# Global attention: two PSUM copies move from ScalarE's queue to VectorE's

## The reference

```
q = rope((x @ Wq).reshape(b, s, 2 * H, hd)); k = rope((x @ Wk).reshape(b, s, 2 * H, hd))   # 32 half heads of 8
v = (x @ Wv).reshape(b, s, H, 2 * hd)                                                      # 16 heads of 16
probs = softmax(einsum('bhqd,bhkd->bhqk', q * hd ** -0.5, k))
w = probs[:, :, 0] - lam * probs[:, :, 1]
attn = einsum('bhqk,bhkd->bhqd', w, v)
attn = attn * rsqrt(mean(attn * attn) + EPS) * subln_g * (1 - LAMBDA_INIT)
return attn.reshape(b, s, -1) @ Wo
```

## Time and profile before

| | us |
|---|---|
| median of 3 runs | 8516.29 (8493.72 to 8532.59) |
| the profiled execution | 8488.95 |
| its span, first to last instruction | 8484.5 |
| PE, DVE, ACT, POOL busy | 7651.8 (90%), 6965.3 (82%), 6290.1 (74%), 3252.0 (38%) |
| of these: DVE's reductions L1440, 4096 | 4707.9 |
| ACT's exponentials L1515, 8192 | 4405.8 |
| ACT's copies L1524 (224) and L1530 (256) | 86.7 and 64.1 |

### The profile page before, as it was taken

The page is one execution under the profiler, slowest core; times in us unless marked ns, Lnnn a source line. Parts: engine busy times, 40 slices in busy tenths (PEclk is TensorE's granted clock), DMA queues, the critical chain, the costliest instruction groups (busy, mean ns, idle before and its releaser), DMA issues. The chain is left out here.

```text
span 8484.5 us, 166411 instructions
## 1 busy us (share of the span) xinstructions
PE 7651.8 (90%) x65584; PEld 2773.6 (33%) x65584; DVE 6965.3 (82%) x8955; ACT 6290.1 (74%) x11674; POOL 3252.0 (38%) x4567
## 2 busy tenths in 40 slices
PE   6899978999789997899988999889998899979999
PEld 3322343223432234322343223432234322343223
DVE  5899768997689976899768997689976899668996
ACT  3699756997569975699756997569975699656996
POOL 3244232442324423344233442334423344234441
PEclk9999989999899998999999999999999999989999
DMA  0100001000010000100001000010000100001000
GB/s 30 46 21 23 17 11 46 21 24 15 11 46 21 24 15 11 46 24 21 15 11 46 25 21 15 11 50 21 22 19 6 50 21 25 18 4 50 22 23 21
DMA packets 219176, 205.43 MB, mean 24 GB/s; under 512 B 108086, under 2 KB 143414, under 8 KB 218358
## 3 DMA queue, kind: packets, MB, share of 16 engines
q1 hardware_dynamic: 218364, 194.46, 8.0%
HBM read 123.83 MB, written 67.37 MB: 23 GB/s over the span
## 5 line engine op out<-in xcount | busy, mean ns | idle before, releaser
L1440 DVE TENSOR_REDUCE mfull<-ps 128x1 f32<-128x1024 f32 x4096 | 4707.9, 1217 | 328.6 <-PE ps L1362 327.7
L1515 ACT ACTIVATE work<-ps 128x512 f32<-128x512 f32 x8192 | 4405.8, 598 | 373.6 <-PE ps L1384 257.5
L1402 PE MATMUL ps<-work,vbuf 128*32 128x256 f32 x32768 | 2624.1, 392 | 119.5 <-ACT hh L1535 119.5
L1362 PE MATMUL ps<-kop,qop 48*128 48x512 bf16 x8192 | 2490.4, 385 | 47.8 <-DVE mfull L1440 24.3
L1384 PE MATMUL ps<-qop,kop 51*128 51x512 bf16 x8192 | 2488.8, 384 | 0.9 <-DMA qop<-mT 0.7
L1402 PEld LDWEIGHTS ps<-work,vbuf 128*32 128x32 f32 x32768 | 654.4, 108 | 1769.3 <-issue 968.2
L1384 PEld LDWEIGHTS ps<-qop,kop 51*128 51x128 bf16 x8192 | 481.6, 93 | 1641.3 <-ACT work L1515 1525.8
L1466 POOL CAST mpart<-mfull 128x16 bf16<-128x16 f32 x256 | 50.4, 197 | 2467.0 <-issue 2004.2
L251 POOL TENSOR_TENSOR rstd<-rstd,nhalf 128x8 f32<-128x8 f32 x64 | 109.3, 1707 | 1632.4 <-DVE rstd L245 1632.4
L1484 POOL TENSOR_TENSOR work<-work,none 128x16 f32<-128x16 f32 x224 | 650.3, 2903 | 18.8 <-POOL mpart L1470 1.5
L450 POOL TENSOR_TENSOR hh<-work,hmask 128x1024 f32<-128x1024 f32 x256 | 520.7, 2062 | 111.4 <-PE ps L382 79.0
(11 more groups left out here) (178 smaller groups left out, 8868.0 us busy)
## 6 DMA issues: line engine op xcount, KB each, us to landing
qop<-scratch SPq DMA_DIRECT2D x512, 64.0 KB
scratch<-work SPq DMA_DIRECT2D x32, 768.0 KB, 4.1
scratch<-hh SPq DMA_DIRECT2D x32, 768.0 KB, 3.6
kop<-scratch SPq DMA_DIRECT2D x256, 96.0 KB
vbuf<-in_x SPq DMA_DIRECT2D x9, 2048.0 KB, 8.3
qop<-scratch SPq DMA_DIRECT2D x512, 32.0 KB
kop<-scratch SPq DMA_DIRECT2D x256, 64.0 KB
qop<-mT SPq DMA_DIRECT2D x1024, 3.0 KB
```

The lines of the kernel that those rows point to most:

```text
L1362: pe.matmul(ps[:, b + n, :], qop[r:r + KQ, s, i, t * P:(t + 1) * P], kop[r:r + KQ, s, i, half(n)], start=True, stop=True).then_inc(s_ms, 1)
L1402: mm = pe.matmul(ps[VW * i:VW * (i + 1), OB, cols], vp[:, b, t, (G * gl + i) // 2, :], prob[:, u % PS, i, cols], start=t == 0 and part == ...
L1440: v.tensor_reduce(mfull[:, m // CUT % 2, r // ROWS * G // 2 + i, to:to + 1], ps[:, b:b + NB, :].rearrange("p b n -> p (b n)"), AX.X, ALU.m ...
L1515: act.activation(prob[:, u % PS, hl, :], ps[:, EB[slot % len(EB)], :], ACT.Exp, scale=scale).then_inc(s_ex, 1)
```

## The change

`keep_raw` and `keep_maxima` leave ACT's queue and stand in DVE's. DVE's loop over the 512 reductions becomes a loop over the clock. In a step it issues `keep_raw` (if an early turn is due), then `reduce(e + 23)`, then `keep_maxima` (if a turn of maxima is due). Early turns get a semaphore of their own, `s_rk`, since `s_ex` now counts ACT's exponentials alone: PE's `bank_for` waits for `s_rk` where the bank's last user was an early turn, and POOL's `early` waits for `s_rk` too. No instruction is removed or added but for the move; bytes, tiles and PE's order stay.

```diff
                     def bank_for(slot):
-                        if slot >= len(EB):
-                            pe.wait_ge(s_ex, slot - len(EB) + 1)
+                        last = slot - len(EB)
+                        if last in TURNS:
+                            pe.wait_ge(s_rk, TURNS.index(last) + 1)
+                        elif last >= 0:
+                            pe.wait_ge(s_ex, last + 1 - sum(1 for s in TURNS if s < last))
                         return EB[slot % len(EB)]
...
                         if part == 0:
-                            pe.wait_ge(s_ex, slot_of(G * (u + 1) - 1) + 1)
+                            pe.wait_ge(s_ex, G * (u + 1))
...
+                    def keep_raw(j):
+                        slot = turn_slot(j)
+                        if j >= 2:
+                            v.wait_ge(s_ch, LINKS * (j - 2) + 2)
+                        v.wait_ge(s_sc, slot + 1)
+                        src = ps[:, EB[slot % len(EB)], :].rearrange("p (k w) -> p k w", w=VW)
+                        v.tensor_copy(raw[j % 2], src[:, :, 0:LD + 1]).then_inc(s_rk, 1)
+
+                    def keep_maxima(h):
+                        v.wait_ge(s_mt, h + 1)
+                        if h >= 1:
+                            v.wait_ge(s_md[(h - 1) // NB % SLOTS], placed(h - 1))
+                        v.tensor_copy(mT[:, :], turn_at(h)[1]).then_inc(s_mts, 1)
+
                     project_dve(v)
-                    for m in range(LAST):
-                        reduce(m)
+                    for e in CLOCK:
+                        if e in EARLY:
+                            keep_raw(EARLY.index(e))
+                        if e + AHEAD < LAST:
+                            reduce(e + AHEAD)
+                        if at(e, TURN) is not None:
+                            keep_maxima(at(e, TURN))
...
-                        pool.wait_ge(s_ex, turn_slot(j) + 1)
+                        pool.wait_ge(s_rk, j + 1)
...
                     for e in CLOCK:
-                        if e in EARLY:
-                            keep_raw(EARLY.index(e))
                         if 0 <= e < LAST:
                             for n in range(NB):
                                 exponentials(NB * e + n)
-                        if at(e, TURN) is not None:
-                            keep_maxima(at(e, TURN))
                         if tile_due(e, 1) is not None and tile_due(e, 1) % T == T - 1:
                             keep_output(tile_due(e, 1))
```

More of the change, by code:

```diff
@@ L1238, in diff_attention @@
             s_ch = sem("da_ch")
+            s_rk = sem("da_rk")
             DMAS = 2 * (len(Q_ROWS) + len(K_ROWS))
@@ L1276, in turn_slot @@
                 return NB * EARLY[j] + j
+            TURNS = [turn_slot(j) for j in range(len(EARLY))]
             def max_bank(m):
@@ L1516, in exponentials @@
                                        ACT.Exp, scale=scale).then_inc(s_ex, 1)
[L1518 to L1530, removed]
                     def keep_output(u):
```

## The result

| | before | changed |
|---|---|---|
| median, us | 8516.07 (8493.72 to 8532.59, 4 runs) | 8663.57 (8661.13 to 8666.80, 4 runs) |
| the profiled execution, us | 8488.95 | 8666.80 |
| its span, us | 8484.5 | 8665.1 |

The ratio is 1.0175, 95% interval 1.0152 to 1.0199: slower by 147 us (129 to 169 by the interval), where 144 was forecast. That the two errors cancel to 3 us is luck.

A forecast was written before the change was run, and what follows sets the result against it. PE was taken to set the pace, with DVE and ACT close behind. The maxima's copy adds 144 us, the early copy, ACT's relief and DVE's amount nothing: 8516 + 144 = 8660 us, range 8600 to 8715.

The forecast's parts named there:

- The bound: Clocked phase: PE sets an ordinary step's pace, 1.11 us; a 16-step cut takes 19.52 us, including events in PE's order.
- Step 1: Maxima's copy behind DVE's reduction of m-1: PE's tile m 0.58 us later, 248 times, +144 us (+114 to +169).
- free by then: At the turn of the maxima, ACT was taken as free when it copies them, 1504.90 to 1505.15.
- Step 2: Early copy, 224 of them, 0.44 us each, fits DVE's hole behind the early turn: nothing, upper end +22 us.
- Step 3: ACT without the two copies, 64.1 + 86.7 us busy: it has slack already, so nothing gained.
- Step 4: DVE's load per cut becomes 18.6 us, under 19.52: not the bound by amount, only by order at one place.
- ACT as the bound: Rival: PE truly waits for ACT, so moving its copies takes 150.8 us off, median 8365 us; chance 0.05.
- Given back: Rival: PE's 0.43 us wait for DVE per turn falls away, leaving +37 us, 8553 us; chance 0.07.
- The early copy that also pushes: Rival: DVE has no hole at the early turn, each of 224 costs 0.35 us: +78 on top, 8738; chance 0.10.
- the signs named in advance: Profile after: cut 20.1 us, PE's copy waits 0.5 to 0.6, turn wait still 0.43, ACT's busy time some 150 us lower.

The follow-up runs named there:

- e1: Changed kernel with the maxima's copy given back to ACT, the early copy left on DVE: 8511.69 us, ratio to before 0.9991.
- e2: Changed kernel with the early copy given back to ACT, the maxima's copy left on DVE: 8672.65 us, ratio to before 1.0181.
- e3: Changed kernel with the maxima's copy put ahead of the reduction of m-1 in DVE's queue: 8520.24 us, ratio to before 1.0009.
- e6: Kernel before, maxima turned behind the step's value products into tile m's second bank, copy wait before the second half: 8473.63 us, ratio 0.9959.
- e5: Kernel before with an extra, unused SBUF copy in ACT's queue ahead of each maxima copy: 8661.46 us, ratio to before 1.0183.
- e4: Changed kernel, maxima turned into tile m's second bank, PE's wait for their copy before the second half: 8588.37 us, ratio to before 1.0090.
- e7: Changed kernel with the maxima copied twice in DVE's queue, first into a spare tile: 8684.89 us, ratio to before 1.0213.

## Why the prediction was right, step by step

**The bound.** It held that PE sets the pace, that DVE and ACT are near it, and that a place in a queue decides and not a sum of busy time. e1 (ACT relieved of 224 copies: nothing), e2 (the loss with 256 short copies on DVE) and e3 (all of DVE's new work and no loss) show it. PE's pace has one part that is DVE's, as the prediction said: the 0.43 us that each turn waits for the reduction of m-2, and e6 gained by filling it. The 1525.8 us of the earlier trace rows, in which PE's weight loads followed an exponential, were no waits that set the time: the row reads 1445.5 us over 3624 loads after the change, 80 us less, while the kernel became 147 us slower.

```profile
PEld ps L1390 <- ACT work L1540: 1445.5, 3624, 1.1
```

**Step 1, the maxima's copy.** Place and chain were right: the copy starts 1.13 after the reduction of m-1, at 572.27 (571.14 + 1.13); PE starts tile m 0.15 after the copy's end (572.47 to 572.62); the second half, the products, DVE's and ACT's next instructions all shift. The mis-sized term was the copy: 0.205 us, not 0.28. So a turn costs 0.49, not 0.58, and the step is 248 x 0.49 = 122 us, not 144. I had chosen the f32 row of 274 ns as the nearest and named the price that the Trainium skill gives (VectorE: DVE Perf Modes, the sections on the TRN2 errata and on the perf-mode tier table), by its formula an estimate of 0.19 us for a 16-bit copy of 128 columns from PSUM. The trace bears the page out within 0.015 us, and the sum by it was 122.

One reading of the kernel before was wrong and harmless: ACT was not "free by then". Its six exponentials run to 1501.73 + 3.28 = 1505.01, and the copy starts at 1504.90, 0.11 before that end, as ACT's exponentials do that stand back to back (0.60 less 0.49). It is 0.15 behind the turn's end (1504.53 + 0.22 = 1504.75), where the idle DVE of e3 started 0.04 behind it. So ACT's copy was held by the instruction in front of it too; that instruction holds the queue for 0.49 us, a reduction for 1.13.

```profile
1501.73 3.28 ACT L1515 ACTIVATE work<-ps 128x512 f32<-128x512 f32 x6
```

**Step 2, the early copy: nothing.** Right: e1, which moves this copy alone, differs from before by 1.6 us. It took 0.432 us where 0.44 was worked out, started at 568.34, 1.13 after the reduction ahead of it, and the reduction followed 568.86 - 568.12 = 0.74 after the step's first score matmul, as before (1502.03 - 1501.29).

**Step 3, ACT: nothing.** Right. ACT's idle time ahead of the exponentials rose from 373.6 to 610.1 us in all; the time freed turned into waiting.

**Step 4, DVE's amount.** 18.6 of 19.52 us a cut were worked out as fitting; e3 ran such a cut in 19.48.

**The rivals.** ACT as the bound is out by e1. Given back is out by the row of PE's waits ahead of the turn, still 0.43 us each (107.6 / 248). The early copy that also pushes is out by e1. Of the signs named in advance, two looked different. ACT's busy time fell by 95 us (6290.1 to 6195.3) and not by some 150: each copy overlapped an exponential by 0.11 us (1501.45 + 0.39 against 1501.73, 1505.01 against 1504.90), time that busy time counts once, and 480 x 0.11 is 53 of the 56 us. And PE's wait for the copy (0.54 us, 572.08 to 572.62) is on no line of the wait list with its full length, since PE's score matmul of the same step runs in it; the timeline shows it.

**What the sum missed.** 248 x 0.49 = 122 us, and the medians are 147 apart (129 to 169), the two profiled executions 178. By the interval the rest of 25 us is barely clear of noise in this pair alone; e2 and e5 have it too (last section). In the trace the clocked phase accounts for 8 x 15.6 = 125 us of this (from first to last turn of a pass 605.2 us before, 620.8 after). The rest lies between the clocked phases, where no instruction was changed but the copy behind a pass's last turn. Three such stretches follow, each from the last turn of one pass to the first of the next, first before, then after.

```profile
956.60:1406.20 449.60, 378.18 (x2167) 192.19 (x2165) 302.68 (x619) 232.09 (x386) 142.97 (x79) 0.92 0.10 30
2011.70:2463.90 452.20, 381.29 (x2167) 193.95 (x2167) 302.55 (x619) 232.12 (x385) 142.97 (x79) 0.91 0.10 30
3069.50:3515.00 445.50, 374.73 (x2167) 189.93 (x2165) 301.34 (x619) 232.00 (x385) 142.83 (x79) 0.93 0.10 30
```

```profile
970.70:1430.90 460.20, 388.89 (x2175) 197.85 (x2171) 303.61 (x620) 232.80 (x385) 142.94 (x79) 0.89 0.10 29
2051.60:2509.50 457.90, 387.08 (x2175) 197.06 (x2175) 303.62 (x621) 232.65 (x385) 142.93 (x79) 0.89 0.10 29
3130.20:3582.90 452.70, 381.57 (x2175) 194.21 (x2175) 303.32 (x621) 232.53 (x385) 142.99 (x79) 0.91 0.10 29
```

DVE, ACT and POOL are as busy as before; PE is busy for longer, at a mean granted clock of 0.89 to 0.91 instead of 0.91 to 0.93. The records of the granted clock hold, per such stretch, 71 us at the 1.2 GHz level before and 87 after; 16 us at half the speed are 8 us, and the stretches are 7.8 us longer on average. So this part of the difference between the profiled executions is PE's granted clock in the other stages. The kernel before varies by itself too (its 19 runs span 8478.77 to 8547.76; the profiled one was among its fastest), so the profiled pair overstates it and the medians, 147 - 122 = 25 us, are the better measure.

## What to carry to other kernels

Moving work to an engine with idle time is safe only if the holes are where the work becomes ready: a copy of 0.43 us was free behind an early turn, a copy of 0.20 us cost 0.49 behind a turn of maxima, on the same engine at the same load, and that one was free again one place ahead. For an instruction that another engine waits for, ask what stands directly in front of it in its in-order queue (here a 1.13 us reduction), and on the waiting engine what stands behind the wait; moving either by one instruction was worth 75 to 143 us here. Of three engines at 92 to 95% busy, compare what one step costs each from start to start (here 1.11 us for PE, 0.98 for ACT, 1.13 for DVE) and look for the holes: DVE, whose pitch is the longest, still waited for PE three times a cut; a wait list that names the last semaphore to come is not evidence for it.

## What was not expected of the hardware

Where the second half of tile m waits for the copy, it started earlier than the handoff of 0.15 us would give: 0.06 after the copy's end in e4, 0.05 in e6. PE's program differs at the two places. Where 0.15 was seen (first half of tile m, turn of the maxima), PE waits for two semaphores; the second half of tile m waits for the copy alone. In the changed kernel's trace the weight load of tile m's first half starts 0.12 after the copy's end (572.47 to 572.59) and the matmul 0.03 after the load; in e4 the load of the second half starts 0.05 after it (572.20 to 572.25) and the matmul 0.01 after the load. So the difference arises mostly before the load, as a second wait would make it; no run varies the number of waits alone.

The time between the clocked phases changed in kernels in which nothing there was touched. With the clocked phase taken from first to last turn, eight times its change leaves these differences between the medians and before: 22 us for the change itself, 37 in e2, 18 in e4, 27 in e5, 23 in e6 (whose phase is shorter), 13 in e7, and 4 and 1 in e3 and e1, whose phases are within 1 us of before. In the profiled executions the stretch between two clocked phases, less half of its time at the lower clock level, is 411.3 to 413.0 us in all nine kernels, against 447.6 to 456.1 as it stands, so there it is the granted clock that differs. Why it is granted lower after a phase of another length stays open; no run here isolates it. In its size, 0.2 to 0.4%, it is near what a measurement of this kernel can tell.
